# Inverse roots of a six-layer stage as one power of -1/2 on GpSimd, with the orders of all four engines written anew

## The chip, the cores and the metric

One core of a Trainium2 chip runs the whole program. The metric is the device time in microseconds of one execution; lower is better. Three executions of the kernel before gave 4577.34, 4577.74 and 4584.95 us, with a median of 4577.74 us.

## The reference

`x` is 4 x 1024 tokens of width 128. After a layernorm without weights, two branches read it, and their results are added to `x`: one causal attention with 16 heads of width 8 (called the attention stage below), and a stack of six layers (the windowed stage). The change is in the windowed stage alone:

```
for i in range(6):
    # attention in windows of 32 tokens, 16 heads of width 64; t is x with half of its features shifted by a token
    q, k, v = split(t @ Wqkv[i], 3)
    q = q / max(norm(q), 1e-12) * q_scale[i];  k = k / max(norm(k), 1e-12) * k_scale[i]
    q = q*cos*scale + rotate_half(q)*sin*scale;  k = k*cos/scale + rotate_half(k)*sin/scale
    x = softmax(mask(q @ k.T * 8)) @ v @ Wo[i] + x      # each window sees itself and the window before
    # feed-forward with a layernorm; t again shifted
    xn = (t - mean) / sqrt(var + 1e-5) * g + b
    a, gate = split(xn @ W1[i] + b1, 2)
    x = a * gelu(gate) @ W2[i] + b2 + x
```

So each token needs 32 inverse norms per layer (16 heads of q, 16 of k) and one inverse standard deviation.

## The kernel before

Everything is 32-bit float except some masks and the attention stage's scores. Four pieces run one after another: `prepare` (layernorm), `attention`, `windowed` (lines 622 to 1597, where the six layers are) and `finish` (transposing back and adding).

In `windowed` the unit of work is a pair of chunks: a chunk is 128 tokens on 128 partitions, a pair is u = 0 and u = 1. There are 16 pairs a layer and 96 in all; the pair number is called r or `pair - n`. Work on heads goes in two halves of 512 columns, i (or e, or par) = 0 and 1. There is no planner in the code. Each engine has its own list, `body(pair)`, written out by hand, and runs the list once per pair in a hardware loop (`over_pairs`). One pass through the list works on several pairs at once: it starts pair - 1, is in the middle of pair - 2 and ends pair - 3. An engine takes its instructions strictly in the order of its list; semaphores hold an instruction until what it reads is there and what it overwrites has been read. `chunk(engine, semaphore, r, u, back=n)` waits for the count that stands for chunk (r, u), n chunks earlier.

The way of a chunk through the engines:

- TensorE projects q, k, v (`project`, line 922) into two PSUM banks `px`, which are shared in the fixed rotation `PX_USES`. ScalarE squares q and k (`square_k`, `square_q`), and copies q and v out. VectorE rotates k (`rotate_k`, `straight_k`, `add_k`), GpSimd rotates q (`straight_q`, `rotate_q`, `add_q`) with the position's table (`tables`), since GpSimd doesn't read PSUM.
- VectorE sums the squares (`sum_k`, `sum_q`) into 32 columns, `ss`. Then comes the inverse root: `clamp` on VectorE (maximum with 1e-24), a logarithm and an exponential with factor -1/2 on ScalarE (`factor_log`, `factor_seed`), and one Newton step in three instructions on VectorE (`refine`, lines 1432 to 1436), which gives `rn`, minus twice the inverse root. GpSimd multiplies q and k by it (`normalise_q`, `normalise_k`), and TensorE transposes them (`turn_q`, `turn_k`) for `scores`.
- Softmax: `max_scores`, `shift_scores` (VectorE), `exps` (ScalarE), `turn_p`, `values` (TensorE), `sum_p`, `invert`, `scale_c` (VectorE), `turn_c`, `project_out`, `add_attention`.
- Feed-forward: `build_xf`, `ffn_turn`, `stats`, `aggregate`, then `var_log` and `var_seed` on ScalarE, and on VectorE four chained small instructions and the normalisation (`normalise_x`, lines 1506 to 1516), `ffn_back`, `scale_xn`, three rounds of `ffn_hidden`, `gelu`, `gate`, then `ffn_out` and `add_ffn`.

The chained small instructions of the feed-forward's normalisation:

```
nc.vector.tensor_tensor(lt[:], ls[:], ls[:], ALU.mult)                                     # L1506
nc.vector.scalar_tensor_tensor(lt[:], mv[:, :, 1], 1e-5, lt[:], ALU.add, ALU.mult)          # L1508
nc.vector.tensor_scalar(lt[:], lt[:], -0.5, 1.5, ALU.mult, ALU.add)                         # L1510
nc.vector.tensor_tensor(lr[:], lt[:], ls[:], ALU.mult)                                     # L1512
```

ScalarE needs another function table for `gelu` than for the exponential and the logarithm: there is one table load at the first `gelu` (L1229) and one right after the third (L1231), where the kernel asks for a table that has both logarithm and exponential.

`prepare` and `attention` compute their inverse roots differently: from an integer guess and three Newton steps, eleven small VectorE instructions (lines 62 to 71, `RSQRT_STEPS = 2 + 3 * 3`).

Of the kernel before, what the change touches and what calls it, by code (L numbers as in the profile page):

```python
# [9 lines left out]

# [1702 lines left out]
```

## Time and profile before

| | |
|---|---|
| median of three executions | 4577.74 us |
| the profiled execution's own time | 4593.52 us |
| its span, first to last instruction | 4591.7 us |
| mean granted TensorE clock | 0.942 of full speed |
| TensorE matmuls, weight loads | busy 4043.8 us (88%), 2700.9 us (59%) |
| VectorE, ScalarE, GpSimd | busy 3732.5 (81%), 2817.7 (61%), 2502.8 us (55%) |
| windowed stage, first to last feed-forward input copied (line 1203) | 997.9 to 4562.0 us, 96 pairs |

Busy time is the time in which an engine has an instruction of its own running; waits and semaphore work don't count. In the rows, PE is TensorE, PEld its weight loads, DVE VectorE, ACT ScalarE, POOL GpSimd. The granted clock is TensorE's: 1.00 is 2.4 GHz, 0.50 is 1.2 GHz.

### The profile page before, as it was taken

How to read it: one execution, taken by the hardware profiler on the slowest of the kernel's cores; microseconds unless marked ns; L12 is line 12 of the kernel's file. 1: busy time of each engine (PE TensorE's matmuls, PEld its weight loads, DVE VectorE, ACT ScalarE, POOL GpSimd, SP SyncE). 2: the span in 40 equal slices, each digit the busy share in tenths (PEclk: the TensorE clock that was granted, in tenths of full speed). 3: DMA queues.
4: the chain of work that ended last, by engine and by line, in shares of the span. 5: the costliest groups of instructions: out<-in, count | busy, mean ns of one | idle time of the engine just before them, and what ended most of it. 6: DMA issues, size and time to landing. Idle time of an engine off the chain costs nothing. (4 is left out here: it accounts for less than half of the span.)

```text
span 4591.7 us, 176379 instructions
## 1 busy us (share of the span) xinstructions
PE 4043.8 (88%) x67601; PEld 2700.9 (59%) x67840; DVE 3732.5 (81%) x7589; ACT 2817.7 (61%) x5554; POOL 2502.8 (55%) x2355
## 2 busy tenths in 40 slices
PE   4588778778999999999999999999999999999997
PEld 2233333346666666666666666666666666666665
DVE  7676566468888888888888888888888888888886
ACT  4154444456666666666666666666666666666664
POOL 4000000056666666666666666666666666666663
PEclk7698898989999999999999999999999999999998
DMA  2322121032222222222222223222232222222221
GB/s 78 47 27 32 22 29 15 11 94 56 56 55 55 66 68 56 57 60 60 74 55 55 55 55 79 59 57 57 55 79 55 55 55 57 69 57 55 55 55 47
DMA packets 176308, 250.44 MB, mean 55 GB/s; under 512 B 46918, under 2 KB 65988, under 8 KB 175300
## 3 DMA queue, kind: packets, MB, share of 16 engines
q1 hardware_dynamic: 176196, 248.94, 22.5%
q8 instruction: 71, 1.16, 0.1%
q14 instruction: 41, 0.34, 0.0%
HBM read 39.08 MB, written 8.39 MB: 10 GB/s over the span
## 5 line engine op out<-in xcount | busy, mean ns | idle before, releaser
L922 PE MATMUL w_px<-w_wqkv,w_xs 128*128 (+1 forms) x2304 | 1164.5, 608 | 61.0 <-DVE w_kr L1414 32.6
L1306 POOL TENSOR_TENSOR w_qr<-w_raw,w_tc 128x512 f32<-128x512 f32 x384 | 486.2, 1277 | 512.9 <-ACT w_raw L1136 333.6
L1313 POOL TENSOR_TENSOR w_qrot<-w_raw,w_tc 128x512 f32<-128x512 f32 x384 | 481.8, 1277 | 451.4 <-ACT w_raw L1136 451.4
L505 ACT ACTIVATE a_probs<-a_wide 128x256 f32<-128x256 f32 (+7 forms) x512 | 309.4, 649 | 401.2 <-PE a_wide L419 397.9
L922 PEld LDWEIGHTS w_px<-w_wqkv,w_xs 128*128 128x128 f32 x2304 | 380.9, 192 | 267.4 <-issue 187.0
L1320 POOL TENSOR_TENSOR w_qr<-w_qr,w_qrot 128x512 f32<-128x512 f32 x384 | 489.6, 1275 | 0.0
L1328 POOL TENSOR_TENSOR w_qr<-w_qr,w_rn 128x512 f32<-128x512 f32 x384 | 402.1, 1047 | 146.1 <-DVE w_rn L1436 138.5
L548 DVE TENSOR_REDUCE a_row_max<-a_ring 128x1 f32<-128x512 f32 (+3 forms) x512 | 298.7, 591 | 210.3 <-PE a_ring L394 116.9
L1336 POOL TENSOR_TENSOR w_kr<-w_kr,w_rn 128x512 f32<-128x512 f32 x384 | 397.3, 1045 | 65.0 <-DVE w_rn L1436 65.0
L1015 PEld LDWEIGHTS w_pw<-w_ot,w_wo 128*128 128x128 f32 x3072 | 368.2, 193 | 61.1 <-issue 50.9
L1015 PE MATMUL w_pw<-w_ot,w_wo 128*128 128x128 f32 x3072 | 387.3, 280 | 5.6 <-issue 4.4
L531 POOL COPY a_v_pad<-a_v_all 128x256 f32 (+1 forms) x16 | 6.4, 402 | 688.5 <-PE a_out L433 688.4
L1182 ACT ACTIVATE w_p<-w_p 128x512 f32<-128x512 f32 x384 | 240.9, 630 | 200.5 <-DVE w_p L1449 200.5
L1524 DVE SCALAR_TENSOR_TENSOR w_hid<-w_pf,w_b,w_gl 128x256 f32<-128x256 f32 (+1 forms) x288 | 138.4, 481 | 276.5 <-ACT w_gl L1229 276.5
L391 PE MATMUL a_ring<-a_k_stack,a_q_stack 96*128 96x512 bf16 (+3 forms) x768 | 262.2, 351 | 108.6 <-DVE a_row_max L548 44.5
L1128 ACT ACTIVATE w_qsq<-w_px 128x512 f32<-128x512 f32 x384 | 227.8, 593 | 210.2 <-PE w_px L922 210.0
L964 PEld LDWEIGHTS w_sc<-w_kt,w_qt 64*32 64x32 f32 x24576 | 263.7, 105 | 88.4 <-issue 86.4
L992 PE MATMUL w_sc<-w_vw,w_pts 64*32 64x64 f32 x24576 | 310.1, 225 | 2.1 <-issue 2.1
L1442 DVE TENSOR_REDUCE w_mx<-w_sc 128x8 f32<-128x512 f32 x384 | 262.3, 683 | 55.6 <-PE w_sc L964 55.6
L964 PE MATMUL w_sc<-w_kt,w_qt 64*32 64x64 f32 x24576 | 297.2, 225 | 4.5 <-issue 4.5
L992 PEld LDWEIGHTS w_sc<-w_vw,w_pts 64*32 64x32 f32 x24576 | 263.3, 105 | 50.8 <-issue 50.8
L1399 DVE TENSOR_TENSOR w_turn<-w_px,w_tc 128x512 f32<-128x512 f32 x384 | 263.6, 686 | 34.3 <-ACT w_ksq L1121 30.9
(154 smaller groups left out, 9558.8 us busy)
## 6 DMA issues: line engine op xcount, KB each, us to landing
w_vw<-w_v SPq DMA_DIRECT2D x1152, 128.0 KB, 2.3
w_vw<-w_v SPq DMA_DIRECT2D x768, 64.0 KB, 2.0
...
```

The lines of the kernel that those rows point to most:

```text
L505: nc.scalar.activation(probs[kc % 2][:, hh, 0:width], wide_bank[w % 2][:, 0:width], ACT.Exp).then_inc(exp_done, 1)
L548: nc.vector.tensor_reduce(into, bank_at(hg, n)[:, 0:width], AX.X, ALU.max).then_inc(r_done, 1)
L922: nc.tensor.matmul(px[bank_of(PX_USES, what, i, u)][:], xs[u][:], rhs, start=True, stop=True).then_inc(done, 1)
L964: mm = nc.tensor.matmul(sc[e][rows, WIN * j:WIN * (j + 1)], qt[u][d, j, rows], kt[u][d, j, BAND * w:BAND * w + WIN], start=False, stop=Tru ...
L992: mm = nc.tensor.matmul(sc[par][rows, at:at + HD], pts[e][keys, n, rows], vw[u][keys, w, at:at + HD], start=True, stop=True, skip_group_ch ...
L1015: mm = nc.tensor.matmul(pw[:, 0:P], wo[:, n, :], ot[n // 4][:, (n % 4) * P:(n % 4 + 1) * P], start=(n == 0), stop=(n == 7))
L1306: nc.gpsimd.tensor_tensor(by_head(qr[i][:]), by_head(raw[i][:]), wide(table(u, Q_COS)), ALU.mult).then_inc(q_straight[i], 1)
L1313: nc.gpsimd.tensor_tensor(halves(qrot[i][:]), swapped(raw[i][:]), split_table(u, Q_SIN), ALU.mult).then_inc(q_rotated[i], 1)
L1320: nc.gpsimd.tensor_tensor(qr[i][:], qr[i][:], qrot[i][:], ALU.add).then_inc(q_added[i], 1)
L1328: nc.gpsimd.tensor_tensor(by_head(qr[i][:]), by_head(qr[i][:]), factor, ALU.mult).then_inc(q_normal[i], 1)
L1336: nc.gpsimd.tensor_tensor(by_head(kr[i][:]), by_head(kr[i][:]), factor, ALU.mult).then_inc(k_normal[i], 1)
L1399: nc.vector.tensor_tensor(halves(turn[i][:]), swapped(px[bank_of(PX_USES, "k", i, u)][:]), split_table(u, K_SIN), ALU.mult).then_inc(k_tur ...
```

## The change

- The sums of squares are clamped on ScalarE: a rectifier of (ss - 1e-24) gives `over`. GpSimd adds 1e-24 and raises the result to the power -1/2 (`refine`, two instructions of 128 x 32). The logarithm, the exponential and the Newton step of the norms go. As `rn` is now the inverse root itself, the exponential of the scores takes the factor 8 and not 8/4.
- The inverse standard deviation is made by `refine_x` on GpSimd: an addition and a power, each 128 x 2. `var_log`, `var_seed` and the four chained instructions in `normalise_x` go.
- GpSimd clears the two semaphores `chain` and `x_chain` before each use and waits for them at 1.
- `sum_k` and `sum_q` wait in addition for the clamp of the chunk before; `clamp` waits for the factors of the chunk before.
- The requests for a table with logarithm and exponential go (before the loop and after the third `gelu`).
- The lists of all four engines are written anew. The loop's body starts at another point of the cycle (before `turn_k(.., 0, 1)`), so that a pass touches five pairs at its ends (`LAG = 5`) and the rotations of the PSUM banks are given from there.

```diff
-        PX_USES = (("v", 1, 0, 1), ("q", 0, 0, 1), ("k", 0, 0, 1), ("k", 1, 0, 1), ("q", 1, 0, 1), ("v", 0, 1, 1),
-        ("v", 1, 1, 1), ("q", 0, 1, 1), ("k", 0, 1, 1), ("k", 1, 1, 1), ("q", 1, 1, 1), ("v", 0, 0, 0))
-        PT_USES = (("pt", 1, 0, 2), ("kt", 1, 1, 2), ("pt", 0, 0, 2), ("kt", 0, 1, 2), ("qt", 0, 1, 2), ("ct", 1, 0, 2),
-        ("qt", 1, 1, 2), ("ct", 0, 0, 2), ("pt", 1, 1, 2), ("pt", 0, 1, 2), ("kt", 1, 0, 1), ("qt", 0, 0, 1),
-        ("kt", 0, 0, 1), ("qt", 1, 0, 1), ("ct", 0, 1, 2), ("ct", 1, 1, 2))
+        PX_USES = (("k", 1, 1, 2), ("q", 1, 1, 2), ("v", 0, 0, 1), ("v", 1, 0, 1), ("q", 0, 0, 1), ("k", 0, 0, 1),
+        ("k", 1, 0, 1), ("q", 1, 0, 1), ("v", 0, 1, 1), ("v", 1, 1, 1), ("q", 0, 1, 1), ("k", 0, 1, 1))
+        PT_USES = (("kt", 1, 0, 2), ("qt", 0, 0, 2), ("kt", 0, 0, 2), ("qt", 1, 0, 2), ("ct", 0, 1, 3), ("ct", 1, 1, 3),
+        ("pt", 1, 0, 2), ("kt", 1, 1, 2), ("pt", 0, 0, 2), ("kt", 0, 1, 2), ("qt", 0, 1, 2), ("ct", 1, 0, 2),
+        ("qt", 1, 1, 2), ("ct", 0, 0, 2), ("pt", 1, 1, 2), ("pt", 0, 1, 2))
...
-        LAG = 4
+        LAG = 5
...
 def body(pair):
+    turn_k(pair - 2, 0, 1)
+    project(pair - 2, 1, "k", 1)
+    values(pair - 3, 1, 1)
+    turn_q(pair - 2, 0, 0)
+    values(pair - 3, 1, 0)
+    turn_k(pair - 2, 0, 0)
+    turn_q(pair - 2, 0, 1)
+    turn_c(pair - 3, 1, 0)
+    project(pair - 2, 1, "q", 1)
+    turn_c(pair - 3, 1, 1)
+    scores(pair - 2, 0)
+    project_out(pair - 3, 1)
+    project(pair - 1, 0, "v", 0)
     project(pair - 1, 0, "v", 1)
     ffn_turn(pair - 3)
     project(pair - 1, 0, "q", 0)
     turn_p(pair - 2, 0, 1)
+    turn_k(pair - 2, 1, 1)
     project(pair - 1, 0, "k", 0)
-    turn_k(pair - 2, 1, 1)
     values(pair - 2, 0, 1)
     turn_p(pair - 2, 0, 0)
     project(pair - 1, 0, "k", 1)
     turn_q(pair - 2, 1, 0)
     turn_c(pair - 2, 0, 1)
     ffn_hidden(pair - 3, 0)
+    project(pair - 1, 0, "q", 1)
     turn_q(pair - 2, 1, 1)
     turn_c(pair - 2, 0, 0)
-    project(pair - 1, 0, "q", 1)
     project(pair - 1, 1, "v", 0)
     ffn_hidden(pair - 3, 1)
     scores(pair - 2, 1)
     ffn_hidden(pair - 3, 2)
+    project_out(pair - 2, 0)
     project(pair - 1, 1, "v", 1)
-    project_out(pair - 2, 0)
     project(pair - 1, 1, "q", 0)
     project(pair - 1, 1, "k", 0)
     turn_p(pair - 2, 1, 1)
+    ffn_out(pair - 3)
     turn_p(pair - 2, 1, 0)
-    ffn_out(pair - 3)
-    turn_k(pair - 1, 0, 1)
-    values(pair - 2, 1, 1)
-    values(pair - 2, 1, 0)
-    turn_q(pair - 1, 0, 0)
-    turn_k(pair - 1, 0, 0)
-    project(pair - 1, 1, "k", 1)
-    turn_q(pair - 1, 0, 1)
-    project(pair - 1, 1, "q", 1)
-    turn_c(pair - 2, 1, 0)
-    turn_c(pair - 2, 1, 1)
-    scores(pair - 1, 0)
-    project_out(pair - 2, 1)
-    project(pair, 0, "v", 0)
...
-def factor_log(r, u):
-    if outside(r):
-        return
-    chunk(act, clamped, r, u)
-    nc.scalar.activation(lnv[:], ssc[:], ACT.Ln).then_inc(logged, 1)
-
-def factor_seed(r, u):
-    if outside(r):
-        return
-    chunk(act, logged, r, u)
-    nc.scalar.activation(seed[:], lnv[:], ACT.Exp, scale=-0.5).then_inc(seeded, 1)
+def clamp(r, u):
+
+    if outside(r):
+        return
+    for i in range(2):
+        chunk(act, k_summed[i], r, u)
+        chunk(act, q_summed[i], r, u)
+    chunk(act, factors_ready, r, u, back=1)
+    nc.scalar.activation(over[:], ss[:], ACT.Relu, bias=less_tiny[:]).then_inc(clamped, 1)
-    nc.scalar.activation(p[e][:], p[e][:], ACT.Exp, scale=SIM_SCALE / 4).then_inc(exped[e], 1)
+    nc.scalar.activation(p[e][:], p[e][:], ACT.Exp, scale=SIM_SCALE).then_inc(exped[e], 1)
...
-    if n == NF - 1:
-        nc.scalar.preload_act_table_set("natural_log_exp_and_others")
...
 def body(pair):
-    exps(pair - 2, 0, 1)
-    factor_seed(pair - 2, 1)
+    square_k(pair - 2, 1, 0)
+    store_p(pair - 3, 1, 1)
+    copy_q(pair - 2, 1, 0)
+    store_p(pair - 3, 1, 0)
+    store_kt(pair - 2, 0, 1)
+    square_k(pair - 2, 1, 1)
+    store_qt(pair - 2, 0, 0)
+    store_kt(pair - 2, 0, 0)
+    store_qt(pair - 2, 0, 1)
+    store_c(pair - 3, 1, 0)
+    square_q(pair - 2, 1, 1)
+    copy_q(pair - 2, 1, 1)
+    store_c(pair - 3, 1, 1)
+    clamp(pair - 2, 1)
     build_xf(pair - 3)
     copy_v(pair - 1, 0, 0)
+    exps(pair - 2, 0, 1)
     copy_v(pair - 1, 0, 1)
-    exps(pair - 2, 0, 0)
     square_q(pair - 1, 0, 0)
     store_p(pair - 2, 0, 1)
+    copy_q(pair - 1, 0, 0)
+    exps(pair - 2, 0, 0)
     square_k(pair - 1, 0, 0)
-    var_log(pair - 3)
-    var_seed(pair - 3)
-    copy_q(pair - 1, 0, 0)
     store_kt(pair - 2, 1, 1)
     store_p(pair - 2, 0, 0)
     square_k(pair - 1, 0, 1)
     store_kt(pair - 2, 1, 0)
+    scale_xn(pair - 3)
     build_xs(pair - 1, 1)
-    scale_xn(pair - 3)
+    store_c(pair - 2, 0, 1)
     store_qt(pair - 2, 1, 0)
-    store_c(pair - 2, 0, 1)
     gelu(pair - 3, 0)
     square_q(pair - 1, 0, 1)
     store_qt(pair - 2, 1, 1)
     copy_q(pair - 1, 0, 1)
     gelu(pair - 3, 1)
+    store_c(pair - 2, 0, 0)
     copy_v(pair - 1, 1, 0)
-    store_c(pair - 2, 0, 0)
     gelu(pair - 3, 2)
-    factor_log(pair - 1, 0)
+    clamp(pair - 1, 0)
+    exps(pair - 2, 1, 0)
     copy_v(pair - 1, 1, 1)
-    factor_seed(pair - 1, 0)
-    exps(pair - 2, 1, 0)
     exps(pair - 2, 1, 1)
+    build_xs(pair, 0)
     square_q(pair - 1, 1, 0)
-    square_k(pair - 1, 1, 0)
-    store_p(pair - 2, 1, 1)
-    copy_q(pair - 1, 1, 0)
-    store_p(pair - 2, 1, 0)
-    store_kt(pair - 1, 0, 1)
-    build_xs(pair, 0)
-    store_qt(pair - 1, 0, 0)
-    store_kt(pair - 1, 0, 0)
-    square_k(pair - 1, 1, 1)
-    store_qt(pair - 1, 0, 1)
-    square_q(pair - 1, 1, 1)
-    copy_q(pair - 1, 1, 1)
-    store_c(pair - 2, 1, 1)
-    store_c(pair - 2, 1, 0)
-    factor_log(pair - 1, 1)
-
-nc.scalar.preload_act_table_set("natural_log_exp_and_others")
...
+def refine(r, u):
+    if outside(r):
+        return
+    pool.sem_clear(chain)
+    chunk(pool, clamped, r, u)
+    nc.gpsimd.tensor_tensor(ssc[:], over[:], tiny[:], ALU.add).then_inc(chain, 1)
+    pool.wait_ge(chain, 1)
+    nc.gpsimd.tensor_tensor(rn[u][:], ssc[:], minus_half[:], ALU.pow).then_inc(factors_ready, 1)
+
+def refine_x(r):
+    if outside(r):
+        return
+    pool.sem_clear(x_chain)
+    wait(pool, f_aggr, 2 * r + 2)
+    nc.gpsimd.tensor_tensor(le[:], mv[:, :, 1], eps[:], ALU.add).then_inc(x_chain, 1)
+    pool.wait_ge(x_chain, 1)
+    nc.gpsimd.tensor_tensor(lr[:], le[:], minus_half[:, 0:2], ALU.pow).then_inc(f_chain, 1)
...
 def body(pair):
+    tables(pair - 2, 1)
+    add_q(pair - 2, 0, 0)
+    add_q(pair - 2, 0, 1)
+    refine(pair - 2, 0)
+    normalise_k(pair - 2, 0, 1)
     normalise_k(pair - 2, 0, 0)
+    normalise_q(pair - 2, 0, 0)
     carry(pair - 2, 0)
-    add_q(pair - 2, 0, 1)
     normalise_q(pair - 2, 0, 1)
+    rotate_q(pair - 2, 1, 0)
+    straight_q(pair - 2, 1, 0)
+    rotate_q(pair - 2, 1, 1)
+    refine(pair - 2, 1)
+    normalise_k(pair - 2, 1, 0)
     straight_q(pair - 2, 1, 1)
-    straight_q(pair - 2, 1, 0)
-    rotate_q(pair - 2, 1, 0)
-    rotate_q(pair - 2, 1, 1)
+    normalise_k(pair - 2, 1, 1)
+    refine_x(pair - 3)
     tables(pair - 1, 0)
-    normalise_k(pair - 2, 1, 1)
     add_q(pair - 2, 1, 0)
-    normalise_k(pair - 2, 1, 0)
+    carry(pair - 2, 1)
     normalise_q(pair - 2, 1, 0)
     add_q(pair - 2, 1, 1)
-    carry(pair - 2, 1)
     normalise_q(pair - 2, 1, 1)
     straight_q(pair - 1, 0, 0)
+    rotate_q(pair - 1, 0, 0)
     rotate_q(pair - 1, 0, 1)
-    rotate_q(pair - 1, 0, 0)
     straight_q(pair - 1, 0, 1)
-    add_q(pair - 1, 0, 0)
-    tables(pair - 1, 1)
-    normalise_q(pair - 1, 0, 0)
-    normalise_k(pair - 1, 0, 1)
...
     chunk(dve, k_squared[i], r, u)
+    chunk(dve, clamped, r, u, back=1)
...
-    wait(dve, f_seeded, r + 1)
+    wait(dve, f_chain, r + 1)
...
 def body(pair):
+    sum_k(pair - 2, 1, 0)
+    sum_q(pair - 2, 1, 0)
+    rotate_k(pair - 2, 1, 0)
+    invert(pair - 3, 1)
+    straight_k(pair - 2, 1, 0)
+    add_ffn(pair - 4)
+    scale_c(pair - 3, 1, 0)
+    add_k(pair - 2, 1, 0)
+    scale_c(pair - 3, 1, 1)
+    rotate_k(pair - 2, 1, 1)
+    sum_k(pair - 2, 1, 1)
+    straight_k(pair - 2, 1, 1)
+    sum_q(pair - 2, 1, 1)
     add_k(pair - 2, 1, 1)
-    clamp(pair - 2, 1)
     max_scores(pair - 2, 0, 1)
+    add_attention(pair - 3, 1)
     shift_scores(pair - 2, 0, 1)
     max_scores(pair - 2, 0, 0)
-    add_attention(pair - 3, 1)
+    stats(pair - 3)
+    sum_p(pair - 2, 0, 1)
+    aggregate(pair - 3)
     shift_scores(pair - 2, 0, 0)
-    refine(pair - 2, 1)
-    sum_p(pair - 2, 0, 1)
-    stats(pair - 3)
+    normalise_x(pair - 3)
+    sum_q(pair - 1, 0, 0)
     sum_p(pair - 2, 0, 0)
-    sum_q(pair - 1, 0, 0)
-    aggregate(pair - 3)
+    rotate_k(pair - 1, 0, 0)
     invert(pair - 2, 0)
-    rotate_k(pair - 1, 0, 0)
     straight_k(pair - 1, 0, 0)
-    normalise_x(pair - 3)
+    scale_c(pair - 2, 0, 1)
+    rotate_k(pair - 1, 0, 1)
     add_k(pair - 1, 0, 0)
-    scale_c(pair - 2, 0, 1)
+    straight_k(pair - 1, 0, 1)
     scale_c(pair - 2, 0, 0)
-    rotate_k(pair - 1, 0, 1)
-    straight_k(pair - 1, 0, 1)
     add_k(pair - 1, 0, 1)
     gate(pair - 3, 0)
     sum_k(pair - 1, 0, 0)
+    sum_q(pair - 1, 0, 1)
     gate(pair - 3, 1)
-    sum_q(pair - 1, 0, 1)
     sum_k(pair - 1, 0, 1)
-    clamp(pair - 1, 0)
     max_scores(pair - 2, 1, 0)
     shift_scores(pair - 2, 1, 0)
     max_scores(pair - 2, 1, 1)
+    gate(pair - 3, 2)
     shift_scores(pair - 2, 1, 1)
-    refine(pair - 1, 0)
-    gate(pair - 3, 2)
+    add_attention(pair - 2, 0)
     sum_p(pair - 2, 1, 1)
-    add_attention(pair - 2, 0)
-    sum_q(pair - 1, 1, 0)
-    rotate_k(pair - 1, 1, 0)
     sum_p(pair - 2, 1, 0)
-    sum_k(pair - 1, 1, 0)
-    invert(pair - 2, 1)
-    add_ffn(pair - 3)
-    straight_k(pair - 1, 1, 0)
-    scale_c(pair - 2, 1, 0)
-    add_k(pair - 1, 1, 0)
-    scale_c(pair - 2, 1, 1)
-    rotate_k(pair - 1, 1, 1)
-    sum_k(pair - 1, 1, 1)
-    straight_k(pair - 1, 1, 1)
-    sum_q(pair - 1, 1, 1)
```

Left out: the allocation and the filling of the new small tiles (`tiny`, `less_tiny`, `minus_half`, `eps`, `over`, `le`), the tiles and functions that go (`var_log`, `var_seed`, VectorE's `clamp` and `refine`), and the same added wait in `sum_q`.

## Rows read from the trace of the kernel before

**Rows 1.** The page: busy time of TensorE and its granted clock in 40 slices.

```profile
PE 4043.8 (88%) x67601; PEld 2700.9 (59%) x67840; DVE 3732.5 (81%) x7589; ACT 2817.7 (61%) x5554; POOL 2502.8 (55%) x2355
PEclk7698898989999999999999999999999999999998
```

**Rows 2.** Windows: stretch, its length; busy us per engine (instructions); granted clock, DMA.

```profile
2150.00:2750.00 600.00, 558.97 (x10497) 395.37 (x10528) 523.12 (x1038) 405.08 (x816) 405.39 (x384) 0.97 0.23 61
...
2499.40:2537.68 38.28, 35.75 (x658) 25.36 (x660) 32.67 (x66) 25.32 (x51) 25.35 (x25) 0.96 0.21 55
2537.68:2574.27 36.59, 34.05 (x658) 23.97 (x660) 32.70 (x65) 25.40 (x51) 25.35 (x25) 1.00 0.22 57
2513.20:2516.60 3.40, 3.40 (x14) 2.94 (x14) 2.59 (x6) 2.34 (x3) 0.64 (x1) 0.53 0.67 169
2549.80:2553.20 3.40, 3.08 (x22) 2.70 (x23) 3.33 (x6) 2.54 (x4) 1.28 (x1) 1.00 0.61 157
```

**Rows 3.** Line 1203, one instruction per pair: shortest/median/longest ns, first and last start.

```profile
L1203 ACT COPY w_xf<-xb x96: 404/405/408, 997.9 to 4562.0; 128x256 f32 x92, 128x256 f32<-128x256 f32 x4
```

**Rows 4.** Waits of TensorE and GpSimd, 2502 to 3967 us: total us, times, longest.

```profile
PE w_pf L1033 <- DVE w_xnt L1515: 59.7, 39, 1.6
PE w_px L922 <- DVE w_kr L1414: 12.7, 36, 0.4
PE w_pt L1003 <- DVE w_cx L1473: 12.5, 39, 0.3
...
POOL w_qrot L1313 <- ACT w_raw L1136: 186.5, 39, 5.5
```

**Rows 5.** Timeline of TensorE in two pairs: start, us, instructions [idle before].

```profile
2513.41 1.06 PE L1045 MATMUL w_pf<-w_xnf,w_w 128*128 128x256 f32 x2
...
2535.53 0.38 PE L953 MATMUL w_sc<-w_mask_bf,w_ident_bf 128*128 x1
...
2544.11 0.60 PE L932 MATMUL w_pt<-ident,w_kr 128*128 128x128 f32 x4
...
2549.80 0.44 PE L1033 MATMUL w_pf<-ident,w_xnt 128*128 128x128 f32 x2 [1.51 <-DVE w_xnt L1515]
...
2551.49 0.60 PE L1045 MATMUL w_pf<-w_xnf,w_w 128*128 128x256 f32 x2
...
2565.30 0.60 PE L932 MATMUL w_pt<-ident,w_kr 128*128 128x128 f32 x4
```

**Rows 6.** Timeline of VectorE and GpSimd in the second of these pairs.

```profile
2546.46 1.18 DVE L1508 SCALAR_TENSOR_TENSOR w_lt<-w_mv,w_lt 128x2 f32<-128x2 f32 x1
2548.02 0.96 DVE L1512 TENSOR_TENSOR w_lr<-w_lt,w_ls 128x2 f32<-128x2 f32 x1
...
2546.34 1.28 POOL L1320 TENSOR_TENSOR w_qr<-w_qr,w_qrot 128x512 f32<-128x512 f32 x1
...
2547.91 1.05 POOL L1328 TENSOR_TENSOR w_qr<-w_qr,w_rn 128x512 f32<-128x512 f32 x1
```

**Rows 7.** Groups by line over the whole span: count, busy us, mean ns, idle before.

```profile
L1306 POOL TENSOR_TENSOR w_qr<-w_raw,w_tc 128x512 f32<-128x512 f32 x384 | 486.2, 1277 | 512.9 <-ACT w_raw L1136 333.6 <-PE w_pt L942 179.3
L1336 POOL TENSOR_TENSOR w_kr<-w_kr,w_rn 128x512 f32<-128x512 f32 x384 | 397.3, 1045 | 65.0 <-DVE w_rn L1436 65.0
...
L1297 POOL TENSOR_TENSOR w_tc<-w_rope_tab,w_scales 128x256 f32 (+1 forms) x192 | 140.9, 734 | 102.5 <-DMA w_scales<-in_L_ffn_k_scale 102.5
L1422 DVE TENSOR_SCALAR w_ssc<-w_ss 128x32 f32<-128x32 f32 x192 | 137.3, 715 | 19.6 <-DVE w_ss L1386 19.6
...
L1231 ACT ACT_TABLE_LOAD x96 | 123.2, 1283 | 1.7
...
L1153 ACT ACTIVATE w_lnv<-w_ssc 128x32 f32<-128x32 f32 x192 | 44.2, 230 | 45.4 <-DVE w_ssc L1422 43.9 <-issue 0.4
```

**Rows 8.** Timeline of GpSimd: an addition and the multiplication that waits for it.

```profile
2530.03 1.27 POOL L1320 TENSOR_TENSOR w_qr<-w_qr,w_qrot 128x512 f32<-128x512 f32 x1
2531.37 1.04 POOL L1328 TENSOR_TENSOR w_qr<-w_qr,w_rn 128x512 f32<-128x512 f32 x1
```

More of the change, by code:

```diff
@@ L9 @@
 from contextlib import ExitStack
+import math
 import numpy as np
@@ L46 @@
 MASKED = -1e30
+NEWTON_AT = 0.5 ** (1 / 3)
 RSQRT_MAGIC = float(0x5F3759DF)
@@ L643, in windowed @@
         ident_bf = sb("ident_bf", [P, P], BF16)
-        eps = sb("eps", [P, 1])
+        tiny = sb("tiny", [P, 2 * HEADS])
+        less_tiny = sb("less_tiny", [P, 1])
+        minus_half = sb("minus_half", [P, 2 * HEADS])
+        eps = sb("eps", [P, 2])
         keep = sb("keep", [P, PAIRS_B])
@@ L656, in windowed @@
         ss = sb("ss", [P, 2 * HEADS])
+        over = sb("over", [P, 2 * HEADS])
         ssc = sb("ssc", [P, 2 * HEADS])
-        lnv = sb("lnv", [P, 2 * HEADS])
-        seed = sb("seed", [P, 2 * HEADS])
-        step = sb("step", [P, 2 * HEADS])
         rn = [sb(f"rn{u}", [P, 2 * HEADS]) for u in range(2)]
@@ L675, in windowed @@
         mv = sb("mv", [P, 2, 2])
-        lv = sb("lv", [P, 2])
-        ls = sb("ls", [P, 2])
-        lt = sb("lt", [P, 2])
+        le = sb("le", [P, 2])
         lr = sb("lr", [P, 2])
@@ L709, in windowed @@
                                                                             sem("xn_ready"))
-        xf_ready = sem("xf_ready")
+        xf_ready, x_chain = sem("xf_ready"), sem("x_chain")
         f_back, xnf_ready = sem("f_back"), sem("xnf_ready")
@@ L739, in _ @@
                 nc.vector.memset(eps[:], 1e-5)
+                nc.vector.memset(tiny[:], 1e-24)
+                nc.vector.memset(less_tiny[:], -1e-24)
+                nc.vector.memset(minus_half[:], -0.5)
                 nc.vector.memset(keep[:, 0:1], 0.0)
@@ L1203, in build_xf @@
                 nc.scalar.copy(xf[:], t.xb[:, bass.ds(col0(r), 2 * P)]).then_inc(xf_ready, 1)
-            def var_log(r):
-                if outside(r):
-                    return
-                wait(act, f_aggr, 2 * r + 2)
-                nc.scalar.activation(lv[:], mv[:, :, 1], ACT.Ln, bias=eps[:]).then_inc(f_logged, 1)
-            def var_seed(r):
-                if outside(r):
-                    return
-                wait(act, f_logged, r + 1)
-                nc.scalar.activation(ls[:], lv[:], ACT.Exp, scale=-0.5).then_inc(f_seeded, 1)
             def scale_xn(r):
@@ L1391, in sum_q @@
                 chunk(dve, q_squared[i], r, u)
+                chunk(dve, clamped, r, u, back=1)
                 nc.vector.tensor_reduce(ss[:, HEADS + 8 * i:HEADS + 8 * i + 8], by_head(qsq[i][:]), AX.X, ALU.add).then_inc(q_summed[i], 1)
@@ L1414, in add_k @@
                 nc.vector.tensor_tensor(kr[i][:], px[bank_of(PX_USES, "k", i, u)][:], turn[i][:], ALU.add).then_inc(k_added[i], 1)
-            def clamp(r, u):
-                if outside(r):
-                    return
-                for i in range(2):
-                    chunk(dve, k_summed[i], r, u)
-                    chunk(dve, q_summed[i], r, u)
-                nc.vector.tensor_scalar(ssc[:], ss[:], 1e-24, None, ALU.max).then_inc(clamped, 1)
-            def refine(r, u):
-                if outside(r):
-                    return
-                chunk(dve, seeded, r, u)
-                for i in range(2):
-                    chunk(dve, k_normal[i], r, u, back=2)
-                    chunk(dve, q_normal[i], r, u, back=2)
-                nc.vector.tensor_tensor(step[:], seed[:], seed[:], ALU.mult).then_inc(chain, 1)
-                wait(dve, chain, 4 * r + (2 * u + 1))
-                nc.vector.tensor_tensor(step[:], step[:], ssc[:], ALU.mult).then_inc(chain, 1)
-                wait(dve, chain, 4 * r + (2 * u + 2))
-                nc.vector.scalar_tensor_tensor(rn[u][:], step[:], -3.0, seed[:], ALU.add, ALU.mult).then_inc(factors_ready, 1)
             def max_scores(r, u, e):
@@ L1504, in normalise_x @@
                     return
-                wait(dve, f_seeded, r + 1)
-                nc.vector.tensor_tensor(lt[:], ls[:], ls[:], ALU.mult).then_inc(f_chain, 1)
-                wait(dve, f_chain, 4 * r + 1)
-                nc.vector.scalar_tensor_tensor(lt[:], mv[:, :, 1], 1e-5, lt[:], ALU.add, ALU.mult).then_inc(f_chain, 1)
-                wait(dve, f_chain, 4 * r + 2)
-                nc.vector.tensor_scalar(lt[:], lt[:], -0.5, 1.5, ALU.mult, ALU.add).then_inc(f_chain, 1)
-                wait(dve, f_chain, 4 * r + 3)
-                nc.vector.tensor_tensor(lr[:], lt[:], ls[:], ALU.mult).then_inc(f_chain, 1)
-                wait(dve, f_chain, 4 * r + 4)
+                wait(dve, f_chain, r + 1)
                 for c in range(2):
```

## The prediction

> **What bounds the kernel now.** I read the page first: TensorE is busy for 88% of the span and its clock stands at nine tenths or more from the tenth slice on, with few exceptions [rows 1]. That is the windowed stage. Then windows over it: in 600 us TensorE is busy for 559, VectorE 523, ScalarE and GpSimd 405 each, at a clock of 0.97 [rows 2]. So TensorE leads, VectorE is not far behind, and the two others have a third of their time free.
>
> The stage repeats one pass per pair, so the unit of my sum is a pair. Line 1203 runs once per pair: (4562.0 - 997.9) / 95 = 37.52 us [rows 3]. Two pairs one after the other are not alike: 38.28 and 36.59 us, with the same work [rows 2]. In both TensorE stands still before line 1033 for some 1.5 us, until the layernorm's result is there. In the long pair the granted clock then is 0.53 for 3.4 us, the lower of its two levels (1.2 GHz), and the same two matmuls of line 1045 take 1.06 us instead of 0.60 [rows 2, 5]. In the short pair the clock stays at 2.4 GHz. The mean of 37.52 says that about 55% of the pairs are long ones ((37.52 - 36.59) / (38.28 - 36.59)).
>
> What TensorE waits for, over 39 pairs: line 1033 for the layernorm 59.7 us = 1.53 us a pair; a projection for `add_k` 0.33; `turn_c` for `scale_c` 0.32 [rows 4]; with 0.2 for `xf` the short pair has 36.59 - 34.05 = 2.54 us without a matmul [rows 2]. Thus a pair holds 34.05 us of matmuls, 2.54 of waits and 0.93 (37.52 - 36.59) lost to the clock. 34.05 is the floor that this change can't lower, since it takes no matmul away.
>
> **The change part by part.** *The layernorm's root.* Today, two VectorE instructions on two elements per partition take 1.18 and 0.96 us. Each ends when the GpSimd instruction beside it ends (2546.34 + 1.28 = 2547.62 against 2546.46 + 1.18 = 2547.64; 2547.91 + 1.05 = 2548.96 against 2548.02 + 0.96 = 2548.98) [rows 6]. So VectorE is held by a running GpSimd instruction when it reads two operands from SBUF, and the chain's 2.7 us (2546.3 to 2549.0) are mostly that. The Trainium skill, in "VectorE: DVE Perf Modes", section "VectorE Performance Modes", says that the second SBUF port of VectorE is shared with GpSimd and that the two block each other. The trace agrees with it (1.18 us for two elements). It has a consequence that can be seen from the lists without it: the long clamp of one chunk (mean 0.715 us, 128x32, [rows 7]) and both held steps leave VectorE, and no instruction of this kind stays in its list, so a long power on GpSimd holds only GpSimd.
>
> VectorE loses 1.43 us of clamps (137.3 / 96 [rows 7]), six Newton instructions and the four-step chain, together 5.4 us by their groups, and gains nothing: 32.7 - 5.4 = 27.3 us a pair. ScalarE loses two logarithms and two exponentials of 0.23 each and two smaller ones, and gains two rectifiers that I put at the logarithm's 0.23 [rows 7]: 25.4 - 0.9 = 24.5 us. Neither binds. In the new list `normalise_x` stands right behind `shift_scores` and long before `rotate_k`. Laid out from the mask matmul of `scores` as zero (2535.53 [rows 5]): scores end at 1.8, `project_out` at 3.7, `add_attention` is done at 4.5 (it now goes ahead of one shift and one max), `xf` at 5.1, `ffn_turn` at 5.8, `stats`, `sum_p` and `aggregate` until 7.3, `refine_x` until 8.0 if GpSimd is there, `normalise_x` until 8.8. TensorE reaches `ffn_back` at 12.2 (today 14.27, less 1.51 of wait and the other waits before it, [rows 5]). So the 1.5 us wait goes with 3 us to spare, and with it what drops the clock. What is late next is `scale_c` for `turn_c`, some 0.2 us; I leave 0.3 us a pair for this and its like.
>
> *The power on GpSimd.* GpSimd is busy 25.35 us a pair [rows 2]. It gains two additions of 128x32, two powers of 128x32 (call one X), and an addition and a power of 128x2. An addition or multiplication costs (1277 - 734) / 256 = 2.1 ns an element and 0.19 us fixed [rows 7], so 0.26 us for 32. Waiting for its own result costs 0.1: the multiplication that waits for an addition starts 1.34 us after it and not 1.23 [rows 8]. Together 0.5 + 0.3 for the two clamped sums, 0.2 + 0.4 for the layernorm's: 1.4 us, plus 2X.
>
> X is what the trace doesn't show. Below, it is one pass like an addition: 0.26 us. Above, I take what is built elsewhere in this program from plain operations: an inverse root of eleven small steps. Eleven passes of 0.26 are 2.8 us, and as a general power is a logarithm and an exponential behind one another I take three such chains as the upper end, 8.6 us. Between them I take one chain, 2.8 us, since it is the one composite root that the program has. The Trainium skill, in "GPSIMD Engine Reference", section "Performance versus the Vector engine", gives about 12 cycles of 1.2 GHz per element for code with branches that depend on data. As an estimate from that page X would be 0.32 us, and the pair about 0.7 us shorter than my sum; no row here shows a power, so it doesn't enter. The same page's section "Engine selection" advises against elementwise work on GpSimd, which speaks against the change; that rule is my third rival in other words.
>
> *Where X lies on the path.* The tightest place is chunk 1: its last sum is done at about 0.8 behind the mask, the rectifier on ScalarE (behind `store_c`) at 1.4, addition and wait 1.8, then X, then `normalise_k`, `straight_q`, `normalise_k` (1.0 + 1.2 + 1.0): ready at 5.1 + X. TensorE wants it for `turn_k(.., 1, 1)` at 8.58 today (2544.11 [rows 5]), and one projection (0.9) and 0.2 of wait earlier then, 7.5. So up to X = 2.4 nothing waits, at 2.8 some 0.4 us. For chunk 0 there is a second place: `rotate_q(.., 0, 1)` waits for `copy_q`, as it does today (186.5 / 39 = 4.8 us a pair [rows 4]); by my layout that comes at 18. Behind it stand 1.2 + 1.2 + 0.7 + 1.2 + 1.2 of q's work and the table, so `refine` starts at 23.6 and `normalise_k` is done at 25.0 + X; TensorE wants `turn_k(.., 0, 1)` at 27.3 (29.8 today, [rows 5], less the 2.5 of waits). Slack 2.3 - X, again 0.5 us too late. The two delays overlap in part. Queued behind them are the other normalisations and transposes, in the order in which TensorE takes them.
>
> *Tables of ScalarE.* Two loads of 1.28 us a pair [rows 7], before the first `gelu` and before the next exponential, as now: no change. *Added waits* of `sum_k`, `sum_q` and `clamp`: each waits for a clamp or factors that by the layout are half a pair old; nothing.
>
> *Sum.* 34.05 + 0.3 + 0.8 = 35.15 us, against 37.52: 2.37 us a pair, 2.37 x 94 = 223 us (the first and last passes are not full). 4593.5 - 223 = 4370 us for an execution like the profiled one; the median stood 15.8 us under it, so **4355 us**, 4.9% less.
>
> **The rivals.**
> 1. *The table for the exponential is loaded once more at the head of each pass*, since nobody asks for it any more. It would stand before `exps(.., 0, 1)`: 1.28 us [rows 7], of which some 0.75 reach `turn_p`. 35.9 us a pair, 4425 us. For it: the requests are gone. Against: at the loop's end the table is already the exponential's.
> 2. *Another wait takes the layernorm's place* on TensorE and the clock still falls in some pairs: VectorE's new list has `scale_c` and `add_k` on the heels of `turn_c` and the projections. 36.9 to 37.5 us: 4520 to 4578 us. For it: three more waits stand in the profile [rows 4]. Against: VectorE gets 5.4 us freer.
> 3. *GpSimd becomes the bound, and the kernel slower.* Its place is the two powers in its list. A pair takes GpSimd 25.35 + 1.4 + 2X, and about 1.9 of waiting for `copy_q` that TensorE's order forces: 28.6 + 2X. That passes 35.15 at X = 3.3 and today's 37.52 at X = 4.5. At 5.6 us (two chains) a pair is 39.8: +2.3 x 94, 4790 us; at 8.6, 45.8 us and 5360. For it: a general power is more than the chain of rows that I took. Against: with X under 3 it is never seen.
> 4. *Same, but between 3.3 and 4.5 us*: faster still, by 0 to 4%, about 4470 us.
>
> **How the numbers follow.** The forecast 0.46 (X up to 3.3), rival 1 0.05, rival 2 0.09 (of it 0.05 within 0.2%), rival 4 0.11, rival 3 0.29 (0.01 of it within 0.2%). Two tenths of a per cent, about 9 us, is what a measurement can tell. Faster 0.46 + 0.05 + 0.04 + 0.11 = 0.66, same 0.06, slower 0.28. Range: below, X = 0.26 and no leftover wait but 0.2 gives 34.25 us a pair, 4270 us. Above, it takes in rival 3 up to X = 5.6, 4790 us; the 0.15 beyond are left out. The forecast's own range is 4270 to 4400.
>
> **What would show it.** Right: no TensorE wait of a microsecond before line 1033's transposes; granted clock 0.99 and more throughout the stage; pairs of 35 us, all alike; VectorE at 27 us a pair; POOL's power instructions under 3 us. Wrong: powers over 4.5 us with GpSimd busy for nearly all of the stage and TensorE waiting for `normalise_k` or `normalise_q`; or three table loads a pair; or the clock still at 0.97.

## The result: 15% slower

The kernel after takes 5281.36 us (median of 4, 5276.94 to 5283.62), the kernel before 4579.33 us in the same comparison. The ratio is 1.153, with a 95% interval of 1.151 to 1.155. The forecast was 4355 us, with a range of 4270 to 4790.

The page of the kernel after, busy time and granted clock:

```profile
span 5279.7 us, 175472 instructions
PE 4310.7 (82%) x67601; PEld 2746.1 (52%) x67840; DVE 3230.2 (61%) x6440; ACT 2804.1 (53%) x5168; POOL 3665.8 (69%) x2931
PEclk7798988899989999899898999999989999899898
```

TensorE has 82% of a longer span where it had 88% [rows 1], VectorE 61% and not 81%. GpSimd went from 2502.8 to 3665.8 us, and still idles for 31% of the span. No engine is near full, so the time lies in waits. The groups of GpSimd (name, shape, count; busy us, mean ns; idle before) say what is new in it:

```profile
L1329 POOL TENSOR_TENSOR w_rn<-w_ssc,w_minus_half 128x32 f32<-128x32 f32 x192 | 1044.0, 5437 | 15.0
L1338 POOL TENSOR_TENSOR w_lr<-w_le,w_minus_half 128x2 f32<-128x2 f32 x96 | 66.8, 696 | 7.5
L1327 POOL TENSOR_TENSOR w_ssc<-w_over,w_tiny 128x32 f32<-128x32 f32 x192 | 48.5, 252 | 1.9 <-ACT w_over L1162 1.7
```

The power of 128x32 takes 5.44 us, twenty times the addition of the same shape (0.25 us). The stage in windows (as in [rows 2]; the last row is one pair), then the line that runs once per pair (as in [rows 3]):

```profile
2150.00:2750.00 600.00, 505.58 (x8741) 337.11 (x8768) 366.06 (x707) 337.06 (x629) 500.00 (x400) 0.91 0.20 51
...
2519.00:2522.50 3.50, 3.50 (x130) 2.83 (x113) 0.42 (x1) 0.90 (x2) 2.78 (x3) 0.58 0.00 0
2536.40:2540.90 4.50, 4.44 (x73) 2.77 (x74) 2.87 (x7) 1.07 (x2) 4.42 (x7) 0.50 0.00 0
2530.30:2576.10 45.80, 38.78 (x657) 25.79 (x658) 27.45 (x54) 25.23 (x47) 37.46 (x31) 0.89 0.18 46
```

```profile
L1206 ACT COPY w_xf<-xb x96: 404/404/406, 1011.3 to 5250.1; 128x256 f32 x91, 128x256 f32<-128x256 f32 x5
```

A pair takes (5250.1 - 1011.3) / 95 = 44.6 us, against 37.5. The clock of the stage is 0.91, where it was 0.97. The waits of the stage (2502 to 3967 us, 33 pairs; compare [rows 4]):

```profile
PE w_pt L937 <- POOL w_kr L1320: 204.4, 65, 3.3
PE w_pt L1008 <- ACT w_kt L1170: 10.9, 33, 0.3
PE w_pf L1030 <- ACT w_xf L1206: 6.8, 33, 0.2
...
DVE w_xnt L1491 <- POOL w_lr L1338: 124.7, 32, 4.0
...
POOL w_qrot L1297 <- ACT w_raw L1141: 187.1, 66, 3.7
POOL w_qr L1290 <- PE w_pt L947: 36.9, 37, 2.1
```

TensorE's wait for the layernorm is gone. In its place it waits twice a pair for `normalise_k`, 204.4 / 33 = 6.2 us, and GpSimd waits 187.1 / 33 = 5.7 us for the copies of q, which depend on TensorE. The timeline shows how the two hold each other (start, us, instructions [idle before]):

```profile
2509.09 5.44 POOL L1329 TENSOR_TENSOR w_rn<-w_ssc,w_minus_half 128x32 f32<-128x32 f32 x1
2514.67 2.04 POOL L1320 TENSOR_TENSOR w_kr<-w_kr,w_rn 128x512 f32<-128x512 f32 x2
...
2515.86 1.11 PE L937 MATMUL w_pt<-ident,w_kr 128*128 128x128 f32 x4 [3.04 <-POOL w_kr L1320]
2516.76 1.91 PE L927 MATMUL w_px<-w_wqkv,w_xs 128*128 x2
...
2525.99 1.28 POOL L1297 TENSOR_TENSOR w_qrot<-w_raw,w_tc 128x512 f32<-128x512 f32 x1 [3.71 <-ACT w_raw L1141]
2527.56 5.44 POOL L1329 TENSOR_TENSOR w_rn<-w_ssc,w_minus_half 128x32 f32<-128x32 f32 x1
...
2536.46 1.11 PE L937 MATMUL w_pt<-ident,w_kr 128*128 128x128 f32 x4 [3.27 <-POOL w_kr L1320]
...
2549.94 1.28 POOL L1297 TENSOR_TENSOR w_qrot<-w_raw,w_tc 128x512 f32<-128x512 f32 x1 [2.38 <-ACT w_raw L1141]
```

The power of chunk 0 ends at 2514.5, TensorE goes on at 2515.9 after 3.04 us of standing, at 1.2 GHz (its four transposes take 1.11 us and the next projection 1.91, where the same take 0.60 and 1.0 to 1.1 at 2.4 GHz). It then makes the projection of q that GpSimd waits for until 2526.0, and only then comes the second power, for which TensorE stands again.

### The profile page after: what moved, and what is told of

Read it like the earlier page. It is cut to its first block and busy times, and to the rows that moved or that the text cites. A ratio compares the mean times of both kernels' runs of the same rounds, so it can differ in the third digit from the quotient of the medians.

```text
span 5279.7 us, 175472 instructions
## 1 busy us (share of the span) xinstructions
PE 4310.7 (82%) x67601; PEld 2746.1 (52%) x67840; DVE 3230.2 (61%) x6440; ACT 2804.1 (53%) x5168; POOL 3665.8 (69%) x2931
## 5 line engine op out<-in xcount | busy, mean ns | idle before, releaser
L927 PE MATMUL w_px<-w_wqkv,w_xs 128*128 (+1 forms) x2304 | 1322.4, 679 | 34.7 <-DMA w_scales<-in_L_ffn_k_scale 19.5
L1329 POOL TENSOR_TENSOR w_rn<-w_ssc,w_minus_half 128x32 f32<-128x32 f32 x192 | 1044.0, 5437 | 15.0
L937 PE MATMUL w_pt<-ident,w_kr 128*128 128x128 f32 x1536 | 297.8, 326 | 607.1 <-POOL w_kr L1320 607.1
L1458 DVE TENSOR_TENSOR w_cx<-w_sc,w_rinv 128x512 f32<-128x512 f32 x384 | 263.0, 685 | 769.8 <-PE w_sc L997 769.8
L937 PEld LDWEIGHTS w_pt<-ident,w_kr 128*128 128x128 f32 x1536 | 200.1, 161 | 721.1 <-POOL w_kr L1320 357.8
L1126 ACT ACTIVATE w_ksq<-w_px 128x512 f32<-128x512 f32 x384 | 229.3, 597 | 527.4 <-PE w_px L927 520.2
L997 PEld LDWEIGHTS w_sc<-w_vw,w_pts 64*32 64x32 f32 x24576 | 307.4, 123 | 305.5 <-issue 305.4
L1170 ACT COPY w_kt<-w_pt 128x512 f32<-128x512 f32 x384 | 223.8, 583 | 412.8 <-PE w_pt L937 412.8
L997 PE MATMUL w_sc<-w_vw,w_pts 64*32 64x64 f32 x24576 | 379.4, 258 | 0.0
L1441 DVE TENSOR_REDUCE w_rs<-w_p 128x8 f32<-128x512 f32 x384 | 253.4, 680 | 101.9 <-ACT w_p L1185 101.9
```

Source lines behind the costliest of these rows:

```text
L927: nc.tensor.matmul(px[bank_of(PX_USES, what, i, u)][:], xs[u][:], rhs, start=True, stop=True).then_inc(done, 1)
L937: mm = nc.tensor.transpose(bank[:, j * P:(j + 1) * P], kr[i][:, j * P:(j + 1) * P], t.ident[:])
L997: mm = nc.tensor.matmul(sc[par][rows, at:at + HD], pts[e][keys, n, rows], vw[u][keys, w, at:at + HD], start=True, stop=True, skip_group_ch ...
L1329: nc.gpsimd.tensor_tensor(rn[u][:], ssc[:], minus_half[:], ALU.pow).then_inc(factors_ready, 1)
```

## The experiments

Two theories at the start. A: the power's 5.44 us is the whole loss, in a loop that passes GpSimd and TensorE in turn. B: the new lists are worse whatever the power costs. All times are medians, beside 4584.5 us (runs 1 to 4) and 4588.7 us (5 to 8) of the kernel before. The kernel after was measured beside 4579.3 us, so a difference between two of these sets can be off by some 10 us.

**1. The power made cheap.**

```diff
-nc.gpsimd.tensor_tensor(rn[u][:], ssc[:], minus_half[:], ALU.pow).then_inc(factors_ready, 1)
+nc.gpsimd.tensor_tensor(rn[u][:], ssc[:], minus_half[:], ALU.mult).then_inc(factors_ready, 1)
```

> The kernel after, with a multiplication in place of the two 128x32 powers (so the norms are not inverted: that part of the computation is left out); the 128x2 power stays. Theory A (the power's 5.44 us, in a loop that goes back and forth between GpSimd and TensorE, is the whole loss): each power becomes 0.26 us, both waits of TensorE for normalise_k go, the clock stays up, a pair takes 34.3 to 35.2 us, 4270 to 4370 us in all. Rival B (the new lists are worse than the old ones whatever the power costs): TensorE keeps waits of a microsecond or more, a pair over 37.5 us, 4580 us or more.

Measured: 4364.69 us, ratio 0.952 [0.950, 0.953]; most pairs take 34.98 us (the distance of two starts of line 1206, as for the pairs below). Its stage in a window:

```profile
2150.00:2750.00 600.00, 587.38 (x11320) 405.90 (x11320) 466.08 (x902) 427.03 (x801) 462.94 (x511) 1.00 0.25 64
```

And what TensorE waited for in these 600 us (17 pairs):

```profile
PE w_pt L1008 <- ACT w_kt L1170: 5.6, 17, 0.3
PE w_pf L1030 <- ACT w_xf L1206: 3.5, 17, 0.2
```

The clock stays at 1.00 and no wait for GpSimd is left. The two powers cost 5281.4 - 4364.7 = 917 us, 44.62 - 34.98 = 9.6 us a pair. B falls as the cause of the loss.

**2. Half of the power.**

```diff
-nc.gpsimd.tensor_tensor(rn[u][:], ssc[:], minus_half[:], ALU.pow).then_inc(factors_ready, 1)
+nc.gpsimd.tensor_tensor(rn[u][:, HEADS:], ssc[:, HEADS:], minus_half[:, HEADS:], ALU.mult)
+nc.gpsimd.tensor_tensor(rn[u][:, 0:HEADS], ssc[:, 0:HEADS], minus_half[:, 0:HEADS], ALU.pow).then_inc(factors_ready, 1)
```

> The kernel after, with the power taken on 16 of the 32 columns and a multiplication on the other 16 (the inverse norm of q is left out). The work between clamp and factors is then about 0.2 + 2.9 = 3.1 us instead of 5.44, near the 2.8 us that the prediction assumed. Theory A (a loop that passes both powers and both engines, so that each microsecond of power counts twice, plus what the clock gives back): 36 to 40 us a pair, 4430 to 4820 us. Rival C (GpSimd's busy time is the bound, 28.6 + 2X, and below that TensorE's 35.2): 34.8 to 35.5 us a pair, 4340 to 4400 us. Rival B (the lists): over 40 us.

Measured: 4558.43 us, ratio 0.994 [0.992, 0.996]; pairs of 37.06 us. The group of the power, and the window of the stage:

```profile
L1330 POOL TENSOR_TENSOR w_rn<-w_ssc,w_minus_half 128x16 f32<-128x16 f32 x192 | 559.1, 2912 | 0.0
```

```profile
2150.00:2750.00 600.00, 563.11 (x10676) 384.36 (x10675) 440.90 (x853) 405.80 (x756) 527.58 (x516) 1.00 0.24 62
```

TensorE's wait for GpSimd in the same stretch:

```profile
PE w_pt L937 <- POOL w_kr L1320: 25.4, 31, 1.0
```

The stretch X is 0.22 + 2.91 = 3.13 us here (multiplication and power), and TensorE waits 25.4 / 31 = 0.82 us on average at the two places. So the slack (the part of X that passes before TensorE wants the result) is 3.13 - 0.82 = 2.3 us on average. The kernel after gives the same: 5.44 - 3.04 = 2.4 us for chunk 0 and 5.44 - 3.27 = 2.2 for chunk 1. The waits here are 1.0 us at the longest, and the clock is at 1.00. C, GpSimd's busy time as the bound, gave 4400 at most and falls.

**3. The power in the old lists.** The kernel before; `refine` on GpSimd is one power, ahead of `normalise_k(pair - 2, 1, 1)` and of `normalise_q(pair - 1, 0, 0)`; `factor_log`, `factor_seed` and the Newton step go:

```diff
+def refine(r, u):
...
+    chunk(pool, clamped, r, u)
+    nc.gpsimd.tensor_tensor(rn[u][:], ssc[:], minus_half[:], ALU.pow).then_inc(factors_ready, 1)
```

> The kernel before with its own lists, and only the norms' roots changed: clamp stays on VectorE, logarithm, exponential and Newton step go, one power on GpSimd ahead of the first instruction that needs it; the layernorm's chain is left as it was. Theory A: two powers of 5.44 us in GpSimd's list, which had 12 us free a pair but waits in it for copy_q; it crosses between the engines as in the kernel after: 43 to 47 us a pair, 5100 to 5480 us. Rival B (the new lists are the loss): 37.5 to 39 us, 4580 to 4720 us.

Measured: 5249.82 us, ratio 1.145 [1.143, 1.147], pairs of 44.4 us. TensorE's wait for GpSimd between 2150 and 2750 us:

```profile
PE w_pt L934 <- POOL w_kr L1322: 107.1, 28, 3.9
```

The same loss without the new lists, again with two waits a pair: they neither cause nor cure it.

**4. Logarithm and exponential in the new lists.** No power of 128x32: `refine` goes from GpSimd's list, and the clamp's place on ScalarE has both functions. The requests for their table come back.

```diff
-chunk(act, factors_ready, r, u, back=1)
-nc.scalar.activation(over[:], ss[:], ACT.Relu, bias=less_tiny[:]).then_inc(clamped, 1)
+for i in range(2):
+    chunk(act, k_normal[i], r, u, back=2)
+    chunk(act, q_normal[i], r, u, back=2)
+nc.scalar.activation(over[:], ss[:], ACT.Ln, bias=tiny[:, 0:1]).then_inc(clamped, 1)
+chunk(act, clamped, r, u)
+nc.scalar.activation(rn[u][:], over[:], ACT.Exp, scale=-0.5).then_inc(factors_ready, 1)
```

> The kernel after with its lists, but the norms' roots by a logarithm and an exponential on ScalarE, one behind the other where the rectifier stood, without a Newton step, and without any power of 128x32; the layernorm's 128x2 power stays. The table with both functions is asked for as before. Theory A: 34.3 to 35.5 us a pair, granted clock 0.99 or more in the stage, 4270 to 4390 us, so faster than the kernel before by some 5%. Rival B: 37 us a pair or more.

Measured: 4377.58 us, ratio 0.954 [0.952, 0.956], pairs of 35.1 us, clock 1.00 in the stage, as expected:

```profile
2150.00:2750.00 600.00, 586.92 (x11176) 403.57 (x11175) 462.34 (x896) 430.48 (x831) 442.36 (x439) 1.00 0.25 64
```

With neither clamp, power nor Newton step the loss is gone.

**5. Work in the waits**, to measure the clock by itself. In `turn_k`, the PSUM bank is claimed first, then filled, and then the wait comes:

```diff
-chunk(pe, k_normal[i], r, u)
 bank_free(pe, PT_USES, "kt", i, u, r)
 bank = pt[bank_of(PT_USES, "kt", i, u)]
+if i == 1:
+    for n in range(24):
+        nc.tensor.transpose(bank[:, (n % 4) * P:(n % 4 + 1) * P], t.ident[:], t.ident[:])
+chunk(pe, k_normal[i], r, u)
```

> The kernel after, with 24 transposes of the identity put in front of turn_k of the keys' half 1 of both chunks, into the PSUM bank that turn_k then overwrites, and ahead of its wait for normalise_k: some 2.6 us of TensorE work inside two waits of 3.0 to 3.3 us. Nothing else changes. Theory A1 (of the 9.8 us a pair that the kernel after is longer than with a multiplication, 6.3 are the two waits and the rest is the clock, which falls after each of them): the clock stays at 2.4 GHz, a pair takes 41.3 to 42.3 us instead of 44.8, 4950 to 5050 us. Rival D (the rest is other waits in the loop between GpSimd and TensorE, the clock costs nothing on it): 44.8 us a pair or more, 5280 us or more.

Measured: 4988.66 us, ratio to the kernel before 1.087 [1.086, 1.089]; pairs of 41.64 us. Window of the stage, TensorE's wait for GpSimd in it, and the added transposes over the whole span:

```profile
2150.00:2750.00 600.00, 575.69 (x10076) 417.77 (x10103) 394.48 (x764) 364.11 (x678) 540.02 (x432) 1.00 0.21 54
```

```profile
PE w_pt L940 <- POOL w_kr L1323: 14.1, 29, 0.7
```

```profile
L937 PE MATMUL w_pt<-ident 128*128 128x128 f32 x4608 | 534.5, 273 | 0.3 <-ACT w_pts L1195 0.3
```

4608 needless transposes make the kernel after 293 us faster: the clock of the stage goes from 0.91 to 1.00. A1 holds and D falls. TensorE is held about as long as before: by 5.6 us of transposes a pair (534.5 / 96) and by what is left of the two waits, 0.49 us each. What comes back is 44.6 - 41.6 = 3.0 us a pair (the expectation had taken 44.8 and 9.8 for a pair's time and loss; the trace has 44.6 and 9.6). TensorE's busy time says nearly the same. For the same matmuls it is busy for 505.58 of 600 us in the kernel after, 37.6 us a pair, and for 587.38 of 600 in experiment 1, 34.2 a pair. So of the 9.6 us, 6.2 are the waits and 3.0 to 3.4 the clock that falls behind them.

**6. The power for chunk 1 alone.**

```diff
-nc.gpsimd.tensor_tensor(rn[u][:], ssc[:], minus_half[:], ALU.pow).then_inc(factors_ready, 1)
+nc.gpsimd.tensor_tensor(rn[u][:], ssc[:], minus_half[:], ALU.pow if u == 1 else ALU.mult).then_inc(factors_ready, 1)
```

> The kernel after with the power for chunk 1 of each pair and a multiplication for chunk 0 (whose norms are not inverted). Theory A2 (each power has its own slack of about 2.35 us up to its own turn_k, and what is over is waited for once per power): one wait of 3.1 us a pair remains, with some 1.7 us of clock behind it: 34.98 + 3.1 + 1.7 = 39.8 us a pair, 4780 to 4840 us. Rival C (GpSimd's list as a whole is the bound, 28.6 us plus both powers = 34.3 here): TensorE's 35.0 us a pair, 4365 us.

Measured: 4909.11 us, ratio 1.070 [1.068, 1.072], pairs of 40.95 us. Again window and wait:

```profile
2150.00:2750.00 600.00, 541.24 (x9666) 368.33 (x9694) 403.49 (x779) 369.18 (x691) 474.73 (x440) 0.92 0.22 56
```

```profile
PE w_pt L937 <- POOL w_kr L1320: 45.7, 14, 3.3
```

One wait a pair remains, of 45.7 / 14 = 3.26 us, though GpSimd now is far from full (475 of 600 us). C falls again. The time is 70 us above what A2 gave: behind the one wait the clock costs 40.95 - 34.98 - 3.26 = 2.7 us and not 1.7. So the waits add up, one per power, while the clock's part doesn't grow in step with them (2.7 us for one wait, 3.0 to 3.4 for two). Nor is it fixed: the first thirteen pairs of the stage took only 38.4 to 40.0 us, with the same wait of some 3.25 us in nearly all of them.

**7. One exchange in the lists of experiment 4.**

```diff
-turn_c(pair - 3, 1, 0)
 project(pair - 2, 1, "q", 1)
+turn_c(pair - 3, 1, 0)
```

> The version with logarithm and exponential on ScalarE in the new lists, with project(q, 1, 1) taken ahead of turn_c(.., 1, 0) on TensorE (as the old lists had it) and square_q ahead of store_c on ScalarE. It aims at the 0.33 us a pair that turn_c waits for store_kt. If the copy is done while the projection runs: 34.8 us a pair, 4345 to 4360 us. If the projection then waits for add_k instead (0.33 us in the kernel before): 35.1 us, 4378 us, no change.

Measured: 4399.57 us, ratio 0.959 [0.958, 0.961]: 22 us slower than experiment 4 and not faster. Pairs of 35.35 us. The wait for `store_kt` went, and in its place stands this one between 2150 and 2750 us (17 pairs):

```profile
PE w_px L927 <- DVE w_kr L1417: 9.1, 17, 0.5
```

The projection waits for `add_k`, as the second of the two expected outcomes has it, but 0.53 us a pair and so longer than the 0.33 before: a loss where no change was expected. The lines above are TensorE's half of the exchange; no run takes it apart from ScalarE's half.

**8. The layernorm's power alone, in the old lists.** The kernel before with one thing of the change:

```diff
-var_log(pair - 3)
-var_seed(pair - 3)
...
-nc.vector.tensor_tensor(lt[:], ls[:], ls[:], ALU.mult).then_inc(f_chain, 1)
...
-nc.vector.tensor_tensor(lr[:], lt[:], ls[:], ALU.mult).then_inc(f_chain, 1)
...
 normalise_k(pair - 2, 1, 0)
+refine_x(pair - 3)
 normalise_q(pair - 2, 1, 0)
```

> The kernel before, lists and norms' roots as they are, with the layernorm's root alone moved to GpSimd (addition and power of 128x2, behind the second normalise_k of chunk 1); its logarithm, exponential and four chained VectorE instructions go. Theory A3 (most of what the new lists win is the 1.5 us wait for the layernorm and the clock that it costs): VectorE is no longer held, ffn_back comes in time, the clock stays up: 35.1 to 35.7 us a pair, 4370 to 4430 us. Rival E (the new lists are needed for it: normalise_x still stands behind the rotation of k): a wait of over 0.7 us stays before ffn_back, the clock still falls in part: 36.3 us or more, 4480 us or more.

Measured: **4321.18 us, ratio 0.941 [0.940, 0.943]**, pairs of 34.54 us: below the expected range, faster than every other kernel here. Its window, TensorE's waits in it (17 pairs), and two groups over the whole span:

```profile
2150.00:2750.00 600.00, 585.80 (x11319) 413.06 (x11352) 526.22 (x1058) 431.31 (x849) 453.92 (x454) 1.00 0.26 64
```

```profile
PE w_px L925 <- DVE w_kr L1413: 5.6, 16, 0.4
PE w_pf L1028 <- ACT w_xf L1206: 3.6, 18, 0.2
```

```profile
L1334 POOL TENSOR_TENSOR w_lr<-w_le,w_minus_half 128x2 f32<-128x2 f32 x96 | 67.4, 702 | 7.5
L1036 PE MATMUL w_pf<-ident,w_xnt 128*128 128x128 f32 x192 | 42.2, 302 | 3.0 <-DVE w_xnt L1506 3.0
```

The wait before the layernorm's transposes is 3.0 us in the whole span, where it was 1.53 a pair [rows 4], and the clock is 1.00. VectorE still is busy for 526 of 600 us and that does no harm. E falls. With the norms' roots made cheap, the new lists give 34.98 us a pair; the old ones with their Newton step give 34.54. So the rewriting of the lists wins nothing over this one step. The old lists with both, this step and cheap roots of the norms, were not measured.

## Why the prediction was wrong

- **What bounds the kernel: right.** Waits and clock made up the difference between 37.52 and some 34.1 us a pair. Experiments 1, 4 and 8 take most of them away, and pairs fall to 35.0, 35.1 and 34.5.
- **The layernorm's root: right, as far as TensorE goes.** Its wait is gone in the kernel after, in experiment 1 and in experiment 8. VectorE's 27.3 us a pair came out as 27.45. "If GpSimd is there" did not hold in the kernel after: the layernorm's power stands behind the long power of chunk 1, and `normalise_x` waits 124.7 / 32 = 3.9 us for it. That costs TensorE nothing there, since it stands still for the same long power itself. How much of the old wait was VectorE held by GpSimd, and how much the rest of the chain, no run separates.
- **X, the step that failed.** The sum took 2.8 us, one chain of eleven passes like an addition, and 0.8 us of waits from it. X is 5.44, and the waits are 6.2 us a pair. 5.44 is within 3% of two such chains (5.6), but nothing here shows that the power is computed like that. The estimate of 0.32 us that the prediction takes from the Trainium skill ("GPSIMD Engine Reference", section "Performance versus the Vector engine") is too short by a factor of seventeen: its price per element for code with branches is not the price of a power, and the measurement decides. The slack is 2.3 us on average (experiment 2), as the prediction had it (2.4 and 2.3). The floor was set somewhat low: with X at a quarter of a microsecond a pair takes 34.98 us, where the lower end of the range had 34.25; a wait of 0.33 us before `turn_c` stayed, and at four of the five changes of layer one pair takes 38 to 42 us. Nothing in the trace showed X; what could be known was that at 4.5 us the gain is gone. A forecast that turns on one unmeasured operation, with a factor of thirty between its bounds, should have had its likeliest value argued from what a general power consists of, which the text did for the upper end and then put aside.
- **"The two delays overlap in part": wrong.** They add. Experiment 6 keeps one power and one wait of 3.26 us; with both there are two.
- **Rival 3 happened, by another mechanism than the one priced.** It named the two powers in GpSimd's list and put 28.6 + 2X = 39.5 us a pair for X = 5.44, some 4760 us. GpSimd's busy time in it was right: 25.35 + 1.4 + 2 x 5.44 = 37.6 us, against 37.2 measured (500 of 600 us, at 44.6 a pair). Its waiting was not: 1.9 us were allowed, and it waits (187.1 + 36.9) / 33 = 6.8 for what comes from TensorE (5.7 for q's copies, 1.1 for transposes), while TensorE stands still twice for GpSimd. The layout of the prediction itself, with the pair of experiment 1, gives 34.98 + 2 (5.44 - 2.3) = 41.3 us. It was carried only to X = 2.8. The rest, up to 44.6, is the clock. For these two reasons the measured time lies above even the 4790 us that the range allowed for X = 5.6.
- **The clock after the new waits: left out.** The prediction counted the clock as a gain that the layernorm's wait gives back, and as no cost of the waits of 3 us in rival 3. Experiment 5 puts it at 3.0 us a pair, some 290 us in all.
- **Rival 1: not so.** There are two table loads a pair as before (L1220 x96 and L1185 x95, 1283 ns each). **Rival 2: not so,** by experiment 1. The added waits of the sums cost nothing that shows.
